# Loading and preparing an attention layer inside the stage before it, a queue flush moved into the middle of a layer, and another order of steps

## What the reference computes

```python
x = x + _L0_xattn_ref(_layernorm(x, axis=-1), ctx_1024, mask_BxS2_bf1, ...)
x = x + _L0_ffn_ref(_layernorm(x, axis=-1), ...)          # experts
x = x + _L1_xattn_ref(_layernorm(x, axis=-1), ctx_1024, ...)
x = x + _L1_ffn_ref(_layernorm(x, axis=-1), ...)          # ternary weights
x = x + _L2_xattn_ref(_layernorm(x, axis=-1), ctx_1024, fside_BxSx2_0, fside_BxSx2_0, ...)
x = x + _L2_ffn_ref(_layernorm(x, axis=-1), ...)          # sum of 8 factors
x = x + _L3_xattn_ref(...)
x = x + _L3_ffn_ref(...)
```

```python
q = (x @ Wq).reshape(b, n, N_HEADS, HEAD_DIM)
k, v = jnp.split(ctx @ Wkv, 2, axis=-1)
q = apply_axial_rope(q, pos_map)      # out = x1*cos - x2*sin, x1*sin + x2*cos
k = apply_axial_rope(k, ctx_pos_map)
logits = jnp.einsum('bqhd,bkhd->bhqk', q, k) * scale
w = jax.nn.softmax(logits, axis=-1)
attn = jnp.einsum('bhqk,bkhd->bqhd', w, v)
return attn.reshape(...) @ Wout + bout
```

## Time and profile before

| what | us |
|---|---|
| median of 3 runs | 3756.95 |
| lowest, highest | 3756.22, 3761.6 |
| time of the profiled execution | 3756.28 |
| its span, first to last instruction | 3753.3 |
| PE busy | 3414.0 (91% of the span) |
| DVE busy | 2365.9 (63%) |
| ACT busy | 1667.5 (44%) |
| POOL busy | 1307.8 (35%) |
| mean granted TensorE clock of the core | 0.96 of full |

### The profile page before, as it was taken

How to read it: one execution, slowest core, us unless ns; L and a number is a source line. 1 busy time by engine, 2 the same in 40 slices (tenths; PEclk the granted TensorE clock), 3 DMA queues, 4 the chain that set the end, 5 groups by cost and what they waited for, 6 DMA issues and landing times.

```text
span 3753.3 us, 62066 instructions
## 1 busy us (share of the span) xinstructions
PE 3414.0 (91%) x23446; PEld 2808.3 (75%) x23446; DVE 2365.9 (63%) x4621; ACT 1667.5 (44%) x3641; POOL 1307.8 (35%) x1239
## 2 busy tenths in 40 slices
PE   7999999959999699987999699997789999999977
PEld 6999999937777456656998545554689999999865
DVE  6677777863323488865443456665667777777766
ACT  5666665521111255542222255554245555555431
POOL 1013334112243588732222346665422222222212
PEclk9999999979999899998999989999889999999989
DMA  3236665024644100002000100000000000000001
GB/s 129 82 137 228 222 222 180 29 112 157 254 154 172 71 24 25 11 5 79 35 23 1 37 3 4 3 4 15 31 7 13 18 18 18 18 7 19 12 1 48
DMA packets 94869, 246.53 MB, mean 66 GB/s; under 512 B 14448, under 2 KB 18672, under 8 KB 89840
## 3 DMA queue, kind: packets, MB, share of 16 engines
q1 hardware_dynamic: 88336, 222.12, 16.9%
q0 software_dynamic: 6240, 20.45, 1.5%
HBM read 364.95 MB, written 70.52 MB: 116 GB/s over the span
## 4 chain that ended last, share of the span: by engine, by line
PE 39%; DVE 6%; issue 3%; POOL 2%; ACT 2%; DMA 0%; SPq 0%; POOLq 0%; DVEq 0%; ACTq 0%
PE banks L104 35%; PE banks L214 4%; ACT P L78 1%; POOL kst L87 0%; DVE xn L92 0%; DVE X L87 0%; DVE st L270 0%; DVE PL L87 0%; DVE X L95 0%; POOL rs L87 0%; DVE KL L95 0%; ACT nkT L81 0%; DVE P L91 0%; POOL CL L87 0%; DVE XL L87 0%
## 5 line engine op out<-in xcount | busy, mean ns | idle before, releaser
L87 DVE TENSOR_TENSOR X<-X,banks 128x512 f32<-128x512 f32 x352 | 240.2, 683 | 189.3 <-PE banks L104 188.9
L98 DVE TENSOR_REDUCE nmx<-banks 128x4 f32<-128x1024 f32 (+2 forms) x256 | 239.3, 956 | 158.1 <-PE banks L104 155.0
L104 PE MATMUL banks<-XH,wqh 128*128 128x256 f32 x1024 | 291.4, 285 | 0.0
L104 PE MATMUL banks<-XL,wqh 128*128 128x256 f32 x1024 | 285.8, 279 | 0.0
L104 PE MATMUL banks<-XH,wql 128*128 128x256 f32 x1024 | 285.6, 279 | 0.0
L104 PE MATMUL banks<-XH,tT 128*128 128x256 f32 x1024 | 248.8, 286 | 13.7 <-issue 6.6
L87 POOL TENSOR_TENSOR slo<-sraw,shi 128x512 fp32r<-128x512 f32 x96 | 126.8, 1321 | 376.4 <-ACT shi L81 352.8
L78 ACT ACTIVATE nPT<-banks 128x1024 f32<-128x1024 f32 x192 | 196.1, 1021 | 129.8 <-PE banks L104 129.4
L104 PE MATMUL banks<-XL,tT 128*128 128x256 f32 x1024 | 247.3, 285 | 0.0
L104 PE MATMUL banks<-woh,OH 128*128 128x512 f32 x512 | 219.2, 428 | 11.6 <-DVE OL L87 10.0
L78 ACT ACTIVATE P<-banks,nb,qst 128x256 f32<-128x256 f32 x256 | 141.3, 561 | 190.7 <-DVE nb L87 190.6
(11 more groups left out here) (433 smaller groups left out, 10500.2 us busy)
## 6 DMA issues: line engine op xcount, KB each, us to landing
WU<-expert_parts SPq DMA_DIRECT2D x39, 4096.0 KB
WD<-expert_parts SPq DMA_DIRECT2D x39, 2048.0 KB
sraw<-in_moe_w SPq DMA_DIRECT2D x96, 256.0 KB, 3.1
expert_parts<-shi SPq DMA_DIRECT2D x96, 256.0 KB
expert_parts<-slo SPq DMA_DIRECT2D x96, 256.0 KB
wqr<-in_L_xattn_Wq SPq DMA_DIRECT2D x16, 512.0 KB, 4.3
wor<-in_L_xattn_Wo SPq DMA_DIRECT2D x16, 512.0 KB, 5.4
sraw<-in_L_ffn_factors SPq DMA_DIRECT2D x32, 256.0 KB, 3.0
```

The lines of the kernel that those rows point to most:

```text
L87: return self.e.tensor_tensor(out, a, b, op)
L98: return self.e.tensor_reduce(out, a, AX.X, op, **kw)
L104: return self.e.matmul(out, l, r, start=start, stop=stop, skip_group_check=skip)
```

## The change

Five things are changed.

1. SP asks for `Wkv` and `Wq` of layer 2 inside the feed forward, when the last ternary piece is made (`tern` at 96), and for `pos`, `Wout` and `bout` when unit 23's `up` is done (`tup` at 96). To make that possible the tiles of layer 2 lie elsewhere: the weights over `raw` and the first half of `T0`, the tables over the first half of `T1`.
2. DVE computes the angles behind unit 25's `down`, with a second argument tile, so that it doesn't wait for ACT between the two.
3. ACT takes the two `Sin` behind unit 31's `up` and starts layer 2 with `ln`.
4. POOL drains its queue once in layer 1, ahead of its `add` of tile 13 (NT - 3).
5. `PLACES[2]` has other places, and the first tiles have shifts of their own (`first` now reads them for layer 2 too).

```diff
-            "s": (-11, -9, -7.5, -5, -3, -0.5, 2, 3.5), "pv": (6, 9.5, 13, 16), "div": (12, 17.5), "mt": (-3.5, 5),
+            "s": (-10, -9, -7.5, -5, -3, -0.5, 2, 3.5), "pv": (6, 9.5, 13, 16), "div": (11.5, 16.5), "mt": (-3.5, 5),
...
+            "q1st": (-3, 0, -1, 0), "k1st": (-8, 2, 0, 1), "low1": (-12, -0.5, -1, 0), "lowq1": (-4.5, 0, 0, 0)}}
...
-            if L == 2:
-                return 0
-            for shift, kinds in (("rows1", "gl ga gn gt"), ("q1st", "qp qb qsq qst"), ("qsc1", "qsc"), ("k1st", "kp kb ksq kst ksc"),
-                                 ("low1", "k0 k1 k2 k3"), ("lowq1", "q0 q1 q2 q3")):
-                if kind in kinds.split() and n < len(at[shift]):
+            for shift, kinds in (("rows1", "gl ga gn gt"), ("q1st", "qp qb qsq qst qrd qrp"), ("qsc1", "qsc"),
+                                 ("k1st", "kp kb ksq kst ksc krd krp"), ("low1", "k0 k1 k2 k3"), ("lowq1", "q0 q1 q2 q3")):
+                if kind in kinds.split() and n < len(at.get(shift, ())):
...
         else:
-            sp.dma(w["pos"][:], self.ins["fside_BxSx2_0"].rearrange("b (t p) c -> p (b t) c", p=128)).then_inc(S["load_a"], 16)
+
+            sp.wait_ge(S["tern"], 96)
             sp.dma(w["wkv"][:], self.ins[pre + "Wkv"]).then_inc(S["n_wkv"], 16)
             sp.dma(w["wq"][:], self.ins[pre + "Wq"]).then_inc(S["n_wq"], 16)
+            sp.wait_ge(S["tup"], 96)
+            sp.dma(w["pos"][:], self.ins["fside_BxSx2_0"].rearrange("b (t p) c -> p (b t) c", p=128)).then_inc(S["load_a"], 16)
...
+            if step == "add" and l1 and t == NT - 3:
+
+                pool.e.drain()
...
+    def act_angles(self, act):
+        S, w = self.S, self.W[2]
+        for c, name in enumerate(("cosT", "sinT")):
+            act.wait_ge(S["ang"], 11 + 7 * c)
+            act.act(w[name][:].rearrange("p t c -> p (t c)"), w[f"rr{c}"][:], ACT.Sin).then_inc(S["act_one"], 1)
+
     def act_narrow(self, act, L):
-        if not l1:
-            for c, name in enumerate(("cosT", "sinT")):
-                act.wait_ge(S["ang"], 11 + 7 * c)
-                act.act(w[name][:].rearrange("p t c -> p (t c)"), w["rr"][:], ACT.Sin).then_inc(S["act_one"], 1)
...
-            if c:
-                dve.wait_ge(S["act_one"], ONE["cos"])
...
-        else:
-            self.dve_angles(dve)
...
+        self.sp_narrow_load(sp, 2)
 
     def pool_ternary(self, pool):
...
+                if u == 31:
+                    self.act_angles(act)
...
+                if u == 25:
+                    self.dve_angles(dve)
...
         self.fence(sp, 4)
         sp.count_on(NARROW_1)
-        self.sp_narrow_load(sp, 2)
         self.sp_narrow(sp, 2)
```

More of the change, by code:

```diff
@@ L1569 @@
             "k1st": (17, -1.5, 11.5, 8, 4), "low1": (-7.5, -7.5), "lowq1": (-20, -4)},
[4 rows of a table removed]
-            "qp": (-41, -39), "qrd": -39, "qrp": -37, "vp": -20, "vb": -18.5, "out": (35, 35.5), "add": 36, "stat": 37.5}}
[4 rows of a table added]
+            "qrd": -39.5, "qrp": -36, "vp": -20, "vb": -19, "out": (34.5, 37), "add": 35.5, "stat": 45.5,
+            "q1st": (-3, 0, -1, 0), "k1st": (-8, 2, 0, 1), "low1": (-12, -0.5, -1, 0), "lowq1": (-4.5, 0, 0, 0)}}
     def narrow_list(self, L):
@@ L1707, in narrow_tiles @@
             sb("wo", [128, 4, 512], F32)
-            over = self.top
+            sb("stq", [128, 1024], F32R)
+            sb("cb2", [128, 2, 512], F32)
+            assert self.top == self.arena + 32768
+            sb("bo", [128, 512], F32)
+            sb("pos", [128, NT, 2], F32)
+            sb("cosT", [128, NT, 8], F32)
+            sb("sinT", [128, NT, 8], F32)
+            over = self.top
+            sb("m2b", [128, 512], F32)
+            w["ang"] = self.at("ang", [128, NT, 2, 4], F32, over)
+            for i, n in enumerate(("kk", "rr0", "rr1")):
+                w[n] = self.at(n, [128, NT * 8], F32, over + 512 * (i + 1))
+            assert self.top <= self.arena + 32768 + 8192
             sb("qT", [128, 2, 8, 256], F32R)
@@ L1711, in narrow_tiles @@
             sb("PT", [128, 3, 2, 2, 256], F32)
-            sb("stq", [128, 1024], F32R)
-            sb("cb2", [128, 2, 512], F32)
         w["cb"] = [cb[0][:, 0, :], cb[0][:, 1, :], w["cb2"][:, 0, :], w["cb2"][:, 1, :]]
@@ L1716, in narrow_tiles @@
         sb("mT", [8, 2, 256], F32R)
-        sb("bo", [128, 512], F32)
+        if l1:
+            sb("bo", [128, 512], F32)
         sb("rec", [128, 256], F32)
@@ L1722, in narrow_tiles @@
         else:
[L1723 to L1729, removed]
             sb("PS", [128, 2, 2, 256], F32)
@@ L2327, in dve_angles @@
             dve.ts(w["ang"][:, :, :, j], w["pos"][:], float(freqs[j]), None, ALU.mult).then_inc(S["ang"], 1)
-        ang, kk, rr = w["ang"][:].rearrange("p t c j -> p (t c j)"), w["kk"][:], w["rr"][:]
+        ang, kk = w["ang"][:].rearrange("p t c j -> p (t c j)"), w["kk"][:]
         c1 = np.float32(6.28125)
@@ L2332, in dve_angles @@
         for c, (quarter, shift) in enumerate(((0.25, np.pi / 2), (0.0, 0.0))):
-            n = 4 + 7 * c
+            n, rr = 4 + 7 * c, w[f"rr{c}"][:]
             dve.wait_ge(S["ang"], n)
```

## The result

| | before | changed |
|---|---|---|
| median, us | 3756.95 | 3725.3 |
| lowest, highest of 5 runs | 3756.22, 3761.6 | 3717.79, 3736.88 |
| ratio to before, 95% interval | | 0.9917 (0.99 to 0.9934) |
| span of the profiled execution | 3753.3 | 3729.0 |
| mean granted clock | 0.96 | 0.962 |

The changed kernel is 31.65 us faster by the medians (24.7 were forecast) and 24.3 by the two profiled spans. That is 0.8%, and the interval leaves out 1. One profile is no fair measure here: the runs of the changed kernel lie 19 us apart, and the profiled one is among its slower. Run again beside some of the experiments it had a median of 3729.69 (3721.28 to 3742.2), ratio 0.992 (0.9902 to 0.9938).

What follows compares the result with a forecast made beforehand. PE bounds layer 2's middle, but its first 78 us hold much less work. Terms -10.3 + 0.3 - 8.5 - 1.0 - 5.2 = -24.7 against 3756.28 gave 3731.6, as median 3732; range 3724 to 3737, with two rivals 3723 to 3741.

Steps and rivals of the forecast that it cites:

- Fence 4, -10.3: Behind fence 4, the first projection starts near 2114.95 instead of 2125.25: 10.3 us less, bounds 9.5 and 10.6.
- Angles in unit 25, +0.3: Feed forward: 18 small DVE instructions moved behind unit 25's `down` cost 0.3 us, bounds 0 and 4.8.
- The fill, -8.5: Start of layer 2, first projection to the `st` called fourth: 8.5 us less, bounds 2 and 13.
- The hand walk at full clock: Fill of layer 2 walked with row durations: 53.9 us instead of 66.5 at full clock, 12.6 less.
- one fall at 3 us and 1 us of missed waits: Fill of layer 2: allowance for one fall of PE's clock, 3 us, and 1 us of missed waits.
- 20 us of it at 1.2 GHz ... cost some 7: Old fill's last 36.0 us: mean clock 0.72, 20 us at 1.2 GHz; the low clock cost some 7 us.
- a clock of 0.5 for more than 10 us of the fill: Fill of layer 2: a clock of 0.5 for over 10 us was named as showing the prediction wrong.
- The first rival: Fill stays slow, by two or more clock falls or the rotations' chain: gain 1 instead of 8.5, 3739.5 us; chance 0.2.
- The middle and the end, -1.0: Layer 2: `out` ahead of a turn saves 0.1 per two passes, 14 times: 1.0 us less, bounds 0 and 2.5.
- Fence 3, -5.2: POOL's long drain is a debt paid once, earlier; fence 3 opens 5.2 us sooner, bounds 0 and 5.4.
- The clearing holds the first rotation: Rival at the start of layer 2: POOL's clearing of `V` holds the first key rotation: 3735 us; chance 0.05.
- The slower rival: Layer 2: `mt` ahead of a score makes PE wait for DVE's maximum every two passes: 3763 us; chance 0.03.

Runs made afterwards that it cites:

- experiment 3: Changed kernel with DVE's angles and ACT's two `Sin` back at the start of layer 2, loads still early: median 3739.28 us, ratio 0.9937.
- experiment 6: Useless matmuls in PE's waits: changed kernel with 23 more, 3723.39 us; with 52 more, 3716.01; with layer 2's old order and 33 more, 3734.46.
- experiments 1 and 2: Changed kernel without POOL's drain in layer 1, 3736.37 us; with five drains in layer 1, 3736.14; with four more inside the experts, 3737.11.

## Why the prediction was right, and where its sizes were off

- **Fence 4, -10.3.** Right: -10.2 in the profile, -9.8 in the second, where the turn ran at low clock (1.09 us instead of 0.63). Loads 2.2, angles the rest. The reading of the 3.94 us as a wait for the clearing is shown by experiment 3.
- **Angles in unit 25, +0.3.** Right: 0.35. They took 4.5 us; the first `thf` came 2.9 late (3.4 forecast), the second 1.3 (1).
- **The fill, -8.5.** Right in its sum, -8.7 and -7.1, with two errors that cancel. The hand walk at full clock gave 53.9; measured 52.25. The term "one fall at 3 us and 1 us of missed waits" was too small: the clock cost 5.5 and 7.1. And "20 us of it at 1.2 GHz ... cost some 7" was the right reading of the old fill: at full clock it takes 8.5 less. So what the order saves at full clock is 5 to 6 us, and the other 3 came of less time at low clock. That the two errors cancel is luck: one of the prediction's own signs of being wrong, a clock of 0.5 for more than 10 us of the fill, did show (some 13 us in the first profile, some 18 in the second, at means of 0.88 and 0.85). The first rival's condition, two falls or more in the fill, was met in the first profile too. Its outcome wasn't: the fill gained 8.7 and not 1, and the clock's share stayed above its 0.8, because the old fill had lost still more to the clock.
- **The middle and the end, -1.0.** The middle's 28.25 and its cause were right (11 times 0.085, 0.9). But the term stopped there: from the fifth `st` to the last `mt` it is 4.65 less. 1.64 of this are two of the last distances between `mt` (25.33 and 23.87 before, 24.38 and 23.18 after), where PE waits less for the maxima's DMA, and 0.4 the very last one (17.41 and 17.01). The prediction had put nothing for the end. The remaining 1.7 are one fall of the clock behind the fifth `st`, which the kernel before had and the changed kernel's two profiles had not (experiment 6). It comes and goes in both orders, so it is no gain of the order; that leaves 3. Old and new order without that fall differ by 2.9 (412.47 against 409.55). PE's waits in the last 75 us, before and changed:

```profile
PE banks L104 <- DMA nqT<-nmT: 3.2, 3, 1.4
```

```profile
PE banks L104 <- DMA nqT<-nmT: 1.5, 3, 0.7
```

- **Fence 3, -5.2.** Right to 0.02, by the debt paid once; shown by experiments 1 and 2. What the debt consists of was open in the prediction and stays open.
- **The clearing holds the first rotation** (the rival at 3735): no. DVE's products beside it take their 0.41, and POOL is 0.05 us late at most.
- **The slower rival**, `mt` making PE wait for `nmx` in every period: it doesn't. Between 2230 and 2530 PE waits for ACT's copies alone.

Put together the profiles give 5.2 + 10.2 - 0.35 + 8.7 + 4.65 = 28.4 us, and 26.4 with the second profile's 9.8, 7.1 and 4.68. The medians say 31.65 and, in the second series, 30.9 (3760.56 against 3729.69). The stretch from `ts` to the last turn took 407.30 and 411.97 in two profiles of the same code (411.02 before), the start up to `ts` 1696.9 to 1709.99 in kernels that differ there in drains at most, and the end 1143.2 to 1149.3. The 3 to 5 us that are left over are less than these; whether the change has a part in them stays open. So the forecast of 24.7 lies within 4 us of what the profiles add up to, and 7 us under the medians.

## What to carry over

When an order is changed to take waits from TensorE, price the clock apart from the waits: take a stretch of the same matmuls before and after, compare busy time with idle time, and put useless matmuls into the waits to learn what the clock alone is worth. Look at the granted clock behind the stretch as well, before a difference there is put down to the order. Look for a drain or a fence that pays for work done long before, and let the engine pay where nobody waits. And look whether VectorE's instructions from SBUF to SBUF fall beside a long one of GpSimd: here one such `tensor_scalar` took 3.72 us instead of 0.41.

## What the runs showed of the hardware

- TensorE's granted clock fell to 1.2 GHz inside the fill, in the first profile twice and in the second once, though behind the first `kp` no wait of PE in it was over 1.70 us. 19 matmuls in the waits and four ahead of the fence kept it at 2.4 GHz: 5.5 to 7.1 us for nothing but work thrown away.
- The spread between runs follows the clock. Of the changed kernel's 11 runs the five fastest (3717.79 to 3725.3) have a mean granted clock of 0.966, the three slowest (3731.09, 3736.88, 3742.2) 0.962, 0.962 and 0.959; a difference of 0.007 in 3725 us is 26 us, and the runs lie 24 apart.
- POOL's first drain behind its 78 indirect transfers takes some 6.4 us for itself, at once (6.44 at 1245.6) as well as 446 us later (7.23 at 1691.8, less the 0.73 of the `nOT` inside it). What it does in that time is open.
- A pair of 64-row matmul groups (score and `st`) costs 0.67 us, the same two apart from each other 0.86. The Trainium skill (TensorEngine Tiling, section "Key Properties") says that a change of tiling mode drains TensorE. That this is the reason for the 0.19 no run here shows: the `st` of the pair has 128-row work behind it too and takes 0.33.
